# A third bank for the rows' sums, late inputs for two batches, 64-row transposes, and a new order at the last batch and the first two experts

## The chip, the cores and the metric

The kernel runs on one core of a Trainium2 chip. The metric is the device time of one execution in microseconds. Before the change the median of three runs is 163.81 us (163.64 to 164.35). About 0.5% (0.8 us) is the least change that a measurement of this kernel can tell.

## The reference

The input x has B = 8 batches of T = 128 tokens with C = 256 channels; a second input v has the same shape.

```python
x = x + wkv(time_decay, time_first, k=layernorm(x), v=ctx)   # a scan over tokens, each channel by itself
h = rmsnorm(layernorm(x)) * norm_w
scores = softmax(h @ gate_w.T)                # 32 experts
w, ids = top_k(scores, 4); w = w / sum(w)     # 4 experts for each token
routed = sum over the 4: w * (silu(h @ w13[e].gate) * (h @ w13[e].up)) @ w2[e]    # F = 128, at most 256 rows for each expert
out = x + layernorm(x) + routed + shared expert(h)
```

Inside wkv each channel keeps two running sums, of exp(k)*v and of exp(k), both decayed from token to token; its result is their quotient, with an extra weight on the token itself. Everything is fp32.

## The kernel before

**First half, batch after batch.** One batch passes through these steps. ScalarE forms `ek` = exp of the normalised x (`exp_k`, L472) and VectorE multiplies by v (`times_v`, L633). TensorE transposes both to channels (`to_channels`, L940). VectorE runs the scan (`scan`, L639) and forms numerator and denominator (`num_den`, L652). ScalarE forms the reciprocal as exp of minus a logarithm (`first_reciprocal`, L484 and L488). VectorE multiplies (`with_reciprocal`, `minus_quotient`, giving Y). TensorE puts x into a PSUM bank `YT` (`residual_in`, L950) and adds Y, turned back to tokens (`to_tokens`, L955). VectorE takes mean and variance of that bank (`stats`, `mean_var`, `variances`), ScalarE makes scale and shift of them (`shifts`, L495 to L503) and writes the normalised row (`normed`, L507) and the residual base (`base`, L512). TensorE transposes the normalised row (`normed_to_channels`, L964), ScalarE copies it (`normed_T`, L518), TensorE forms the logits (`logits`, L977), VectorE picks four experts and a one-hot table (up to `one_hot`), TensorE counts earlier picks (`slots_so_far`, `positions`, L984 to L993), and VectorE turns the counts into row numbers (`picked_slots`, `slot_sums`, `slot_numbers`, L722 to L733). GpSimd then scatters the batch's rows to DRAM with one indirect DMA for each of the four ranks (`scatter`, L370).

**What sets the order.** Each engine has its own list of (lag, stage) pairs, given to `run`: in round n it carries out each stage for batch n - lag, in the order of the list. So an engine in round n works on several batches at once, and a stage that waits holds up all that stands behind it on that engine. Nothing is reordered by the program; a wait is always on a semaphore that another engine counts up. Buffers come in pairs (index j = batch modulo 2), `YT` among them, and `residual_in` of batch b must wait until ScalarE has finished `base` of batch b - 2.

**Scales of the inputs.** Mean and variance of x are formed before its exponentials: VectorE's `first_stats` (L599, L602), ScalarE's `first_scales` (L452, L454), VectorE's `first_shift` (L594). They come in two groups, batches 0 and 1, then batches 2 to 7. The second group's statistics and shift stand in VectorE's round 0, and its scales in ScalarE's `exp_k` of batch 2, in that round too.

**SP queue.** SP issues all large loads: x, gate weights and v of batches 0 and 1; x and v of batches 2 to 7; eight transfers of 1056 KB that clear the experts' rows in DRAM (L259); the shared expert's weights (L263 to L265); expert weights. GpSimd's scatters of batch 0 wait for the first four clearing transfers, those of batch 1 for the others. An expert's rows are loaded back (`xg`, L273) when rank 0, 0 to 1, 0 to 2 or all ranks have landed, for experts 0, 1, 2 and the rest in the order of work. GpSimd scatters ranks 0 and 1 of the last batch before ranks 2 and 3 of the last two.

**Second half, expert after expert.** For each of 32 experts: TensorE transposes its gathered rows (`rows_to_channels`, L1041), ScalarE copies them (`rows_to_sbuf`, L539), TensorE forms gate and up (`gate_up`, L1055), ScalarE silu (L544), VectorE the product (`gated`, L867), TensorE the down product (`down`, L1072), VectorE copies the result out (L873 to L877), GpSimd scatters it (L384). Counts decide at run time, by branches on TensorE, how many rows an expert has: up to 128 (one half), up to 192 (`second` set) or up to 256 (`third` set too). VectorE carries bookkeeping between the first experts (`picks_of_single`, `picks_of_pair`, `late_picks`, `weights_in_order`). The shared expert's products (`shared_part`, L998; `shared_down`, L1031) lie between the halves. At the end the experts' rows are gathered back by rank, weighted and added.

## Time and profile before

| what | value |
|---|---|
| median of 3 runs | 163.81 us (163.64 to 164.35) |
| the profiled execution, its own time | 165.11 us |
| its span, first to last instruction | 163.3 us |
| TensorE busy | 135.1 us (83% of the span) |
| VectorE busy | 114.1 us (70%) |
| ScalarE busy | 91.4 us (56%) |
| GpSimd busy | 85.5 us (52%) |
| mean DMA rate | 285 GB/s |

The profiled execution took 165.11 us, of which 163.3 us is the span and 1.8 us lies around it. Busy shares are means over stages that differ: the batches take about the first 62 us, then come some 15 us of transition, the experts to 142 us, and the gathering to the end. In the rows below PE is TensorE, PEld its weight loads, DVE VectorE, ACT ScalarE, POOL GpSimd. An fp32 product counts as two records, an fp32 transpose as one. A record's length contains its latency, so that overlapping records are longer than the distance between their starts.

### The profile page before, as it was taken

The numbers are of one execution on the slowest core, as the hardware profiler recorded it, in microseconds if no ns is written. First come the engines' busy times: TensorE is split into PE (matmuls) and PEld (weight loads), VectorE is DVE, ScalarE is ACT, GpSimd is POOL, SyncE is SP. The second block draws the span as 40 slices with busy tenths as digits, with TensorE's granted clock in tenths as the row PEclk, the third lists the DMA queues.
The fourth block names the chain that finished last, engine by engine and source line by source line (L and its number), as shares of the span: only waits on it lengthen the run. The fifth ranks groups of instructions, "written<-read, shape, count | busy, mean of one in ns | idle before, by whom it ended". The sixth has DMA issues, their size and how long they took to land.

```text
span 163.3 us, 2856 instructions
## 1 busy us (share of the span) xinstructions
PE 135.1 (83%) x740; PEld 114.9 (70%) x740; DVE 114.1 (70%) x415; ACT 91.4 (56%) x262; POOL 85.5 (52%) x106
## 2 busy tenths in 40 slices
PE   0254598889886799597979999998999999999591
PEld 0233397879775787285869988987999989888350
DVE  0489989999998633516997788787766787734471
ACT  3623777877777624025847798887845776210011
POOL 8200004777777774720557767777664677671000
PEclk9999999999999999969999999999999999999999
DMA  4999999999999981679989999997766321285977
GB/s 103 288 379 420 420 417 412 385 382 370 375 382 373 373 293 72 151 218 291 365 250 332 381 351 377 366 342 237 209 197 166 118 87 64 69 308 180 354 270 257
DMA packets 32433, 46.49 MB, mean 285 GB/s; under 512 B 3017, under 2 KB 27285, under 8 KB 32156
## 3 DMA queue, kind: packets, MB, share of 16 engines
q1 hardware_dynamic: 27936, 37.15, 67.3%
q0 software_dynamic: 3888, 8.53, 14.4%
q10 hardware_dynamic: 588, 0.54, 1.0%
q8 instruction: 11, 0.18, 0.5%
q14 instruction: 10, 0.08, 0.1%
HBM read 27.95 MB, written 20.48 MB: 297 GB/s over the span
## 4 chain that ended last, share of the span: by engine, by line
PE 53%; DVE 15%; DMA 12%; ACT 9%; issue 6%; POOL 1%; ACTq 1%; SPq 0%; DVEq 0%; POOLq 0%
PE bank L1055 20%; PE bank L1072 11%; PE bank L1041 6%; DMA w_all<-rows_out 5%; DVE S L639 4%; DVE ND L652 2%; PE bank L940 2%; DMA rows_out<-w_all,pick_idx 2%; PE bank L977 2%; PE bank L964 2%; PE bank L955 2%; PE bank L950 2%; DMA xg<-rows_in 2%; ACT n_row L507 2%; ACT ln_den L484 2%
## 5 line engine op out<-in xcount | busy, mean ns | idle before, releaser
L384 POOL DMA_INDIRECT rows_out<-w_all,pick_idx x49 | 48.2, 985 | 28.9 <-DVE w_all L873 10.0
L370 POOL DMA_INDIRECT rows_in<-n_row,slot_all x32 | 32.7, 1023 | 32.3 <-DVE slot_all L733 21.5
L1055 PE MATMUL bank<-xT,w_all 128*128 128x128 f32 (+2 forms) x256 | 41.3, 305 | 1.5 <-issue 1.2
L1055 PEld LDWEIGHTS bank<-xT,w_all 128*128 128x128 f32 x256 | 36.1, 193 | 4.1 <-issue 3.7
L539 ACT ACTIVATE xT<-bank,nws 128x256 f32<-128x256 f32 x64 | 26.9, 471 | 14.9 <-PE bank L1041 14.6
L1072 PE MATMUL bank<-w_all,act_t 128*128 128x256 f32 x92 | 25.3, 382 | 1.0 <-DVE act_t L867 1.0
L867 DVE TENSOR_TENSOR act_t<-sg,bank 128x256 f32<-128x256 f32 x32 | 13.4, 419 | 13.7 <-ACT sg L544 13.6
L544 ACT ACTIVATE sg<-bank 128x256 f32<-128x256 f32 x32 | 12.3, 383 | 9.5 <-PE bank L1055 8.7
L1072 PEld LDWEIGHTS bank<-w_all,act_t 128*128 128x128 f32 x92 | 15.6, 191 | 2.5 <-issue 1.7
L1041 PE MATMUL bank<-ident,xg 128*128 128x128 f32 x92 | 15.8, 280 | 1.5 <-DMA xg<-rows_in 1.4
L1041 PEld LDWEIGHTS bank<-ident,xg 128*128 128x128 f32 x92 | 12.1, 143 | 5.4 <-issue 2.5
L873 DVE COPY w_all<-bank 128x512 f32<-128x512 f32 x17 | 11.7, 687 | 0.7 <-PE bank L1072 0.5
L998 PE MATMUL bank<-hT,sgu 128*128 128x256 f32 x32 | 11.5, 517 | 0.0
L914 DVE SCALAR_TENSOR_TENSOR base_all<-w_all,base_all 128x256 f32<-128x256 f32 x16 | 7.0, 482 | 5.5 <-DMA w_all<-rows_out 5.3
L484 ACT ACTIVATE ln_den<-ND,inv_top 128x128 f32<-128x128 f32 x16 | 5.6, 394 | 9.3 <-DVE ND L652 9.3
L955 PE MATMUL bank<-minus,Y 128*128 128x128 f32 x32 | 8.7, 425 | 2.4 <-DVE Y L669 2.4
L639 DVE TENSOR_TENSOR_SCAN S<-decay,bank 128x512 f32<-128x512 f32 x8 | 9.7, 1213 | 1.3 <-PE bank L940 1.3
L964 PE MATMUL bank<-ident,n_row 128*128 128x128 f32 x16 | 5.5, 448 | 5.5 <-ACT n_row L507 5.5
L1119 PE MATMUL bank<-w_all,v_all 128*128 128x256 f32 x32 | 8.4, 400 | 1.9 <-DMA w_all<-rows_out 1.8
L955 PEld LDWEIGHTS bank<-minus,Y 128*128 128x128 f32 x32 | 7.8, 333 | 2.8 <-DVE Y L669 2.8
L950 PE MATMUL bank<-x_all,ident 128*128 128x256 f32 x16 | 9.3, 686 | 0.0
L940 PE MATMUL bank<-ident,ek 128*128 128x128 f32 x16 | 5.4, 440 | 4.7 <-DVE ekv L633 4.7
(143 smaller groups left out, 228.7 us busy)
## 6 DMA issues: line engine op xcount, KB each, us to landing
w_all<-in_L_ffn_w_dram SPq DMA_DIRECT2D x12, 1024.0 KB, 14.3
rows_in<-w_all SPq DMA_DIRECT2D x8, 1056.0 KB, 16.1
xg<-rows_in SPq DMA_DIRECT2D x32, 264.0 KB, 4.7
w_all<-rows_out SPq DMA_DIRECT2D x2, 1024.0 KB, 5.4
w_all<-rows_out SPq DMA_DIRECT2D x2, 512.0 KB, 7.1
w_all<-rows_out SPq DMA_DIRECT2D x4, 256.0 KB, 8.0
rows_out<-w_all,pick_idx POOLq DMA_INDIRECT x49, 2.9
x_all<-in_x_dram SPq DMA_DIRECT2D x1, 768.0 KB, 6.1
```

The source lines that it names most:

```text
L370: pool.indirect_dma_start(rows_in, bass.IndirectOffsetOnAxis(ap=slot_all[:, b, k:k + 1], axis=0), n_row[:, b, :], None)\
L384: pool.indirect_dma_start(rows_out, bass.IndirectOffsetOnAxis(ap=pick_idx[:, e, a:a + 1], axis=0), yo[e][:, a, :], None, bounds_check=PICK ...
L539: last = act.activation(xT[:, j, h, :], FX[j][:, h, :], ACT.Copy, scale=nws[:, h:h + 1])
L544: act.activation(sg[:, j, :], FG[j][:, 0, :], ACT.Silu).then_inc(s["f_s"], 1)
L639: dve.tensor_tensor_scan(S[:, j].rearrange("p a h t -> p (a h t)"), decay[:, :, :, :].rearrange("p a h t -> p (a h t)"), XT[j].rearrange(" ...
L867: dve.tensor_tensor(act_t[:, j, :], sg[:, j, :], FG[j][:, 1, :], ALU.mult).then_inc(s["f_a"], 1)
L873: dve.tensor_copy(yo[e], FY[i % 2]).then_inc(s["f_yo"], 1)
L950: nc.tensor.matmul(YT[j], ident[:, :], x_all[:, b, :], start=True, stop=False)
L955: last = nc.tensor.matmul(YT[j][:, h * P:(h + 1) * P], Y[:, j, h, :], minus[:, :], start=False, stop=(h == HC - 1))
L1041: last = nc.tensor.transpose(FX[j][:, h, a * P:(a + 1) * P], xg[e % XB][:, a, h * P:(h + 1) * P], ident[:, :])
L1055: last = nc.tensor.matmul(FG[j][:, a, lo:lo + slots], w13_all[:, expert(e), h, a, :], xT[:, j, h, lo:lo + slots], start=(h == 0), stop=(h ...
L1072: return nc.tensor.matmul(FY[j][:, a, :], act_t[:, j, a * P:(a + 1) * P], w2_all[:, expert(e), :], start=True, stop=True)
```

## The change

Seven edits go together.

1. **Third bank.** `YT` gets banks 2, 3 and 5 (batch modulo 3), and the transposed normalised rows `NT` keep one bank instead of two. In TensorE's list `residual_in` moves from the head of the round (for batch n) to behind `positions` (for batch n + 1), and it now waits for `base` of batch b - 3.
2. **Late inputs.** x and v of batches 6 and 7 are loaded by two transfers of their own behind the eight clearing ones. Their statistics and shift move to VectorE's round 4, their scales to ScalarE's `exp_k` of batch 6.
3. **First exponential.** `exp_k` of batch 0 is issued right behind the first scales; VectorE's wait for all constants moves from before the first product to `num_den` of batch 0, and TensorE's wait for the gate weights to the first logits.
4. **Shifts.** In `shifts`, `nb2`, for which `normed` waits, comes before `one_rs2`, for which `base` waits.
5. **Last batch.** `to_tokens` of batch 7 comes before `normed_to_channels` of batch 6. Of the shared expert's products one stands before the last logits instead of two, and none before the last `positions` instead of one; those moved come later. Each half of the logits waits for its own half of the copied rows.
6. **First two experts.** TensorE transposes experts 0 and 1 and then forms gate and up of both; ScalarE copies both before its first silu. Half of the second `shared_down` moves ahead of the first transposes.
7. **64-row transposes.** Where an expert has 129 to 192 rows, the extra half is transposed as 64 rows, behind one more branch.

```diff
-        YT = [bank[2 + j][:, 0:C] for j in range(2)]
-        NT = [bank[4 + j][:, 0:C].rearrange("p (h t) -> p h t", h=HC) for j in range(2)]
+        YT = [bank[q][:, 0:C] for q in (2, 3, 5)]
+        NT = bank[4][:, 0:C].rearrange("p (h t) -> p h t", h=HC)
...
+            sp.dma_start(x_all[:, THIRD:B, :], xv[:, THIRD:B, :]).then_inc(s["x2_in"], 16)
+            sp.dma_start(v_all[:, THIRD:B, :], vv[:, THIRD:B, :]).then_inc(s["v2_in"], 16)
             sp.dma_start(sgu[:, :, 0, :], sh_gate.rearrange("(h p) f -> p h f", p=P)).then_inc(s["sh_in"], 16)
...
             first_scales(0, 0, FIRST)
+            def first_exp():
+                act.wait_ge(s["nb1_done"], 1)
+                act.activation(ek[:, 0, :], x_all[:, 0, :], ACT.Exp, bias=nb1[:, 0:1], scale=rstd1[:, 0:1]).then_inc(s["ek_ready"], 1)
+
+            first_exp()
...
             def exp_k(b, j):
+                if b == 0:
+                    return
                 if b == FIRST:
-                    first_scales(1, FIRST, B)
-                act.wait_ge(s["nb1_done"], 1 if b < FIRST else 2)
+                    first_scales(1, FIRST, THIRD)
+                if b == THIRD:
+                    first_scales(2, THIRD, B)
+                act.wait_ge(s["nb1_done"], 1 if b < FIRST else 2 if b < THIRD else 3)
...
             rows_to_sbuf(0, 0)
-            for e in range(E):
-                if e == 0:
-                    silu(0, 0)
+            rows_to_sbuf(1, 1)
+            silu(0, 0)
+            silu(1, 1)
+            for e in range(1, E):
...
             def others_shift(b, j):
                 if b == 0:
-                    first_shift(1, FIRST, B)
+                    first_shift(1, FIRST, THIRD)
+                if b == THIRD - 2:
+                    first_shift(2, THIRD, B)
...
             def to_tokens(b, j):
+                if b < B - 1:
+                    rows_of(b, j)
+
+            def last_to_tokens(b, j):
+                if b == B - 1:
+                    rows_of(b, j)
...
                     pe.wait_ge(s["sh_in"], 32)
-                    for h in range(HC):
-                        shared_part(0, 0, h)
-                pe.wait_ge(s["hT_ready"], HC * (b + 1))
+                    shared_part(0, 0, 0)
...
                 for h in range(HC):
+                    pe.wait_ge(s["hT_ready"], HC * b + h + 1)
                     last = nc.tensor.matmul(LG, hT[:, b, h, :], gwT[:, h, :], start=(h == 0), stop=(h == HC - 1))
...
-            run([(0, residual_in), (2, slots_so_far), (-1, to_channels), (2, positions), (1, normed_to_channels), (0, to_tokens), (1, logits)])
...
+            run([(2, slots_so_far), (-1, to_channels), (2, positions), (-1, residual_in), (0, last_to_tokens),
+                 (1, normed_to_channels), (0, to_tokens), (1, logits)])
+
+            shared_part(0, 0, 1)
...
-            for h in range(1, HC):
+            for h in range(HC):
+                shared_part(0, 1, h)
+            pe.wait_ge(s["base_ready"], B)
+            for h in range(HC):
                 shared_part(1, 0, h)
...
             pe.wait_ge(s["sdn_in"], 16)
-            shared_down(0)
+            shared_down(0, 0)
+            shared_down(0, 1)
+            shared_down(1, 0)
...
+            def transpose_rows(e, j, a, lo, hi):
                 for h in range(HC):
-                    last = nc.tensor.transpose(FX[j][:, h, a * P:(a + 1) * P], xg[e % XB][:, a, h * P:(h + 1) * P],
-                                               ident[:, :])
+                    last = nc.tensor.transpose(FX[j][:, h, a * P + lo:a * P + hi], xg[e % XB][lo:hi, a, h * P:(h + 1) * P],
+                                               ident[lo:hi, lo:hi])
                 return last
...
+                first_rows = (0, MORE - P) if more else (2 * P - MORE, P)
                 with pe.If(second != 0):
-                    transpose_half(e, j, extra(expert(e)))
-                transpose_half(e, j, main(expert(e))).then_inc(s["f_xt"], 1)
+                    with pe.If(third != 0):
+                        transpose_rows(e, j, more, 0, P)
+                    with pe.Else():
+                        transpose_rows(e, j, more, *first_rows)
+                transpose_rows(e, j, main(expert(e)), 0, P).then_inc(s["f_xt"], 1)
...
+            rows_to_channels(0, 0, second(0), third(0))
+            shared_down(1, 1)
+            rows_to_channels(1, 1, second(1), third(1))
+            gate_up(0, 0, second(0), third(0))
+            gate_up(1, 1, second(1), third(1))
+            for e in range(1, E + 1):
```

On TensorE, one round in the middle of the batches, before the change (`ek` and `ekv` are the exponentials and their products with v, `slot`, `earlier` and `onehot` belong to the counting):

```order
L950 MATMUL bank<-x_all,ident 128x256 [waits base_ready]
L984 MATMUL bank<-slot,ident 128x32 [waits earlier_done,picked_done]
L986 MATMUL bank<-earlier,ones 128x32 x4
L940 MATMUL bank<-ident,ek 128x128 [waits col0_done,nd_done,ekv_ready]
L940 MATMUL bank<-ident,ek 128x128
L940 MATMUL bank<-ident,ekv 128x128 x2
L993 MATMUL bank<-onehot,tri 128x32 [waits onehot_done]
L993 MATMUL bank<-onehot,tri 128x32 x3
L964 MATMUL bank<-ident,n_row 128x128 [waits hT_ready,n_ready]
```

and after it:

```order
L1013 MATMUL bank<-slot,ident 128x32 [waits earlier_done,picked_done]
L1015 MATMUL bank<-earlier,ones 128x32 x4
L958 MATMUL bank<-ident,ek 128x128 [waits col0_done,nd_done,ekv_ready]
L958 MATMUL bank<-ident,ek 128x128
L958 MATMUL bank<-ident,ekv 128x128 x2
L1020 MATMUL bank<-onehot,tri 128x32 [waits onehot_done]
L1020 MATMUL bank<-onehot,tri 128x32 x3
L970 MATMUL bank<-x_all,ident 128x256 [waits base_ready]
L992 MATMUL bank<-ident,n_row 128x128 [waits hT_ready,n_ready]
```

The product that brings x into the bank now stands behind the transposes of the next batch and the counting, directly ahead of the transposes of the normalised rows.

On VectorE in round 4 after the change, from the product with the reciprocal to the next scan (`nb` is the shift of batches 6 and 7 and is new here; before the change nothing stood between `slot_v` and `earlier`):

```order
L681 TENSOR_TENSOR NR<-ND,R 128x512 [waits y_ready,nd_done,r0_ready]
L741 TENSOR_TENSOR picked<-onehot,bank 128x128 [waits pos_ready]
L688 SCALAR_TENSOR_TENSOR Y<-NR 128x256 [waits x1_ready,nr_done]
L747 TENSOR_REDUCE slot_v<-picked 128x4 [waits picked_done]
L607 SCALAR_TENSOR_TENSOR nb<-mv,rstd 128x2 [waits rstd1_done,mv1_done]
L734 TENSOR_TENSOR earlier<-earlier,onehot 128x128 [waits pos_ready,onehot_done]
L752 SCALAR_TENSOR_TENSOR slot_all<-slot_v 128x4 [waits slot_v_done]
L656 SCALAR_TENSOR_TENSOR S<-decay,bank 128x512 [waits nd_done,xt_ready]
```

The shift waits for `rstd1_done`. ScalarE counts that up in the same round at this place (`hT` is the copy of the transposed normalised rows):

```order
L519 ACTIVATE n_row<-bank,nb,rs 128x256 [waits nb2_done]
L524 ACTIVATE base_all<-bank,nb,one_rs 128x256 [waits one_rs2_done]
L530 ACTIVATE hT<-bank,nws 128x128 [waits nt_ready]
L530 ACTIVATE hT<-bank,nws 128x128
L455 ACTIVATE ln_ve<-mv,eps 128x2 [waits mv1_done]
L457 ACTIVATE rstd<-ln_ve 128x2 [waits ln_ve1_done]
L484 ACTIVATE ek<-x_all,nb,rstd 128x256 [waits xt_ready,nb1_done]
```

So the two small instructions stand behind both halves of `hT` of batch 3.

## Rows read from the trace of the kernel before

**Rows 1.** Windows: length, busy PE, PEld, DVE, ACT, POOL, clock, DMA, GB/s.
```profile
36.50:41.95 5.45, 4.96 (x28) 4.46 (x27) 5.11 (x20) 4.26 (x14) 4.23 (x5) 1.00 1.08 376
...
70.00:72.00 2.00, 2.00 (x6) 1.27 (x5) 0.21 (x1) 0.84 (x2) 0.49 (x1) 0.50 0.50 187
...
77.00:150.00 73.00, 70.96 (x448) 63.63 (x447) 54.73 (x199) 46.79 (x121) 48.25 (x49) 1.00 0.75 243
```

**Rows 2.** Chain that ended last, kernel start: start us, us, what.
```profile
6.62 0.53 ACT ek L472
...
11.43 1.98 DVE st L599 x6
...
13.53 0.41 DVE mv L602 x5
```

**Rows 3.** Timeline, VectorE: start us, us, instruction; scans of batches 3 and 7.
```profile
25.63 1.21 DVE L639 TENSOR_TENSOR_SCAN S<-decay,bank 128x512 f32<-128x512 f32 x1
...
47.42 1.21 DVE L639 TENSOR_TENSOR_SCAN S<-decay,bank 128x512 f32<-128x512 f32 x1
```

**Rows 4.** The same chain, TensorE at 33 us: residual product.
```profile
33.07 1.01 PE bank L950 x2
```

**Rows 5.** Timeline around 34 to 37 us; in brackets idle before and releaser.
```profile
34.11 0.16 DVE L680 BATCH_NORM_AGGREGATE mv<-st 128x2 f32<-128x6 f32 x1
...
35.53 0.29 DVE L722 TENSOR_TENSOR picked<-onehot,bank 128x128 f32<-128x128 bf16 x1 [0.20 <-PE bank L993]
...
36.07 0.28 DVE L728 TENSOR_REDUCE slot_v<-picked 128x4 f32<-128x128 f32 x1
...
36.81 0.63 ACT L518 ACTIVATE hT<-bank,nws 128x128 f32<-128x128 f32 x2 [0.33 <-PE bank L964]
```

**Rows 6.** Timeline, ScalarE at the start: scales of batches 2 to 7.
```profile
13.97 0.30 ACT L452 ACTIVATE ln_ve<-mv,eps 128x6 f32<-128x6 f32 x1 [1.57 <-DVE mv L602]
...
14.30 0.21 ACT L454 ACTIVATE rstd<-ln_ve 128x6 f32<-128x6 f32 x1
```

**Rows 7.** Timeline, GpSimd: scatters of rows to the experts.
```profile
37.73 0.96 POOL L370 DMA_INDIRECT rows_in<-n_row,slot_all  x1 [0.30 <-issue]
...
60.29 0.96 POOL L370 DMA_INDIRECT rows_in<-n_row,slot_all  x1 [0.30 <-issue]
...
63.21 0.95 POOL L370 DMA_INDIRECT rows_in<-n_row,slot_all  x1 [1.96 <-issue]
```

**Rows 8.** Timeline, VectorE: row numbers of the last batch.
```profile
61.90 0.16 DVE L733 SCALAR_TENSOR_TENSOR slot_all<-slot_v 128x4 int32<-128x4 f32 x1
```

**Rows 9.** SP queue's timeline; then DMA table: KB each, us to landing.
```profile
15.45 2.35 SPq L263 DMA_DIRECT2D sgu<-L_ffn_shared_gate_w_dram  x1
...
sgu<-L_ffn_shared_gate_w_dram SPq DMA_DIRECT2D x1, 128.0 KB, 16.4
```

**Rows 10.** The chain again, TensorE in the last batch.
```profile
57.13 1.71 PE bank L998 x4
...
60.07 1.04 PE bank L998 x2
```

**Rows 11.** Timeline, TensorE and VectorE, where the experts start.
```profile
66.98 1.10 PE L1031 MATMUL bank<-sdn,act_t 128*128 128x256 f32 x4 [1.11 <-DVE act_t L754]
...
68.99 1.05 PE L1041 MATMUL bank<-ident,xg 128*128 128x128 f32 x4 [0.90 <-DMA xg<-rows_in]
...
74.24 0.44 PE L1041 MATMUL bank<-ident,xg 128*128 128x128 f32 x2 [0.45 <-DMA xg<-rows_in]
...
76.99 0.42 DVE L867 TENSOR_TENSOR act_t<-sg,bank 128x256 f32<-128x256 f32 x1 [0.83 <-ACT sg L544]
...
83.35 0.70 PE L1072 MATMUL bank<-w_all,act_t 128*128 128x256 f32 x2 [0.84 <-DVE act_t L867]
```

**Rows 12.** Timeline, TensorE, logits of one batch.
```profile
32.00 1.06 PE L977 MATMUL bank<-gwT,hT 128*128 128x32 f32 x4
```

**Rows 13.** Instructions by form, 68 to 143 us: busy us, mean ns | idle.
```profile
L1055 PE MATMUL bank<-xT,w_all 128*128 128x192 f32 x104 | 19.9, 335 | 0.4 <-issue 0.4
```

More of the change, by code:

```diff
@@ L235, in _ @@
             vv = ctx_in.rearrange("b t c -> t b c")
[L236 removed]
+            for lo, hi, x_in, v_in in ((0, FIRST, "x0_in", "v0_in"), (FIRST, THIRD, "x1_in", "v1_in")):
                 sp.dma_start(x_all[:, lo:hi, :], xv[:, lo:hi, :]).then_inc(s[x_in], 16)
@@ L1026, in third, with shared_down, rows_to_channels @@
                 return flags[1][expert(e) // BITS] & (1 << expert(e) % BITS)
-            def shared_down(c):
-                pe.wait_ge(s["sh_a"], c + 1)
-                for a in range(2):
-                    last = nc.tensor.matmul(FY[c][:, a, :], act_t[:, c, a * P:(a + 1) * P], sdn[:, :], start=True, stop=True)
-                last.then_inc(s["sh_y"], 1)
+            def shared_down(c, a):
+                if a == 0:
+                    pe.wait_ge(s["sh_a"], c + 1)
+                product = nc.tensor.matmul(FY[c][:, a, :], act_t[:, c, a * P:(a + 1) * P], sdn[:, :], start=True, stop=True)
+                if a == 1:
+                    product.then_inc(s["sh_y"], 1)
             pe.wait_ge(s["sdn_in"], 16)
-            shared_down(0)
+            shared_down(0, 0)
+            shared_down(0, 1)
+            shared_down(1, 0)
             pe.wait_ge(s["nd_done"], 2 * B)
             pe.wait_ge(s["idx_done"], B)
-            def transpose_half(e, j, a):
+            def transpose_rows(e, j, a, lo, hi):
                 for h in range(HC):
-                    last = nc.tensor.transpose(FX[j][:, h, a * P:(a + 1) * P], xg[e % XB][:, a, h * P:(h + 1) * P],
-                                               ident[:, :])
+                    last = nc.tensor.transpose(FX[j][:, h, a * P + lo:a * P + hi], xg[e % XB][lo:hi, a, h * P:(h + 1) * P],
+                                               ident[lo:hi, lo:hi])
                 return last
-            def rows_to_channels(e, j, second):
+            def rows_to_channels(e, j, second, third):
                 pe.wait_ge(xg_in[e % XB], 16 * (e // XB + 1))
+                more = extra(expert(e))
+                first_rows = (0, MORE - P) if more else (2 * P - MORE, P)
                 with pe.If(second != 0):
-                    transpose_half(e, j, extra(expert(e)))
-                transpose_half(e, j, main(expert(e))).then_inc(s["f_xt"], 1)
+                    with pe.If(third != 0):
[3 more added lines that the diff above has]
+                transpose_rows(e, j, main(expert(e)), 0, P).then_inc(s["f_xt"], 1)
             def gate_up_slots(e, j, slots):
@@ L1081, in down @@
                 down_half(e, j, main(expert(e))).then_inc(s["f_y"], 1)
-            rows_to_channels(0, 0, second(0))
-            shared_down(1)
-            for e in range(E + 1):
-                if e == 0:
-                    gate_up(0, 0, second(0), third(0))
+            rows_to_channels(0, 0, second(0), third(0))
[4 more added lines that the diff above has]
+            for e in range(1, E + 1):
                 if e + 1 < E:
-                    rows_to_channels(e + 1, (e + 1) % 2, second(e + 1))
+                    rows_to_channels(e + 1, (e + 1) % 2, second(e + 1), third(e + 1))
                 if e == 1:
```

60 lines of the change are left out of this document (31 added, 29 removed).

## The prediction

> **What bounds the kernel now.** I read the windows first, then the chain of waits, then the timeline where stages meet. Between 36.5 and 41.95 us one batch passes; VectorE is busy for 5.11 of 5.45 us, TensorE for 4.96, ScalarE for 4.26 [rows 1]. So VectorE is the bound of the batches, with 0.34 us of idle time in each. From 77 to 150 us TensorE is busy for 70.96 of 73 us [rows 1]. The four scans from batch 3 to batch 7 start 21.79 us apart, 5.45 for each batch [rows 3].
>
> Between the halves the chain goes through GpSimd. It issues the scatters at 37.73, ..., 60.29 us, with 17 others between, each with only 0.3 us idle before it, and then has a hole of 1.96 us before 63.21 [rows 7]. The last row numbers are written at 61.90 to 62.06 us, 1.15 us before that scatter starts [rows 7, 8]. The first expert's transposes start at 68.99 us, 5.78 after it [rows 11].
>
> **The change part by part.**
>
> *First exponential, -0.6.* It starts at 6.62 us [rows 2], after six small ScalarE instructions. Its shift is ready at about 5.9, so it can start at about 6.0. Bounds 0 and -0.7. The work now behind it is next needed at the first numerator, over 3 us later.
>
> *Fewer statistics at the start, -0.8.* The chain holds six of each kind, 1.98 + 0.41 = 2.39 us [rows 2]. A third of that goes.
>
> *Third bank, -1.5 by the scan of batch 7.* The product that brings x in costs 1.01 us on the chain [rows 4], between the logits and the transposes for a later batch. It moves to where TensorE waits for the normalised rows. VectorE's wait for the counts (0.20 us at 35.53 [rows 5]) then ends. VectorE itself can't go faster than about 5.15 us for each batch, so the gain is 5.45 - 5.15 = 0.3 for each of the five rounds from batch 2 to batch 7. Bounds 0 and -1.7 (5 times the idle 0.34). Putting `nb2` first saves 0.1 on a chain that is then hidden.
>
> *Late statistics, +0.85.* Two of each kind plus a shift return in round 4, on the engine that is the bound.
>
> *The late shift's wait, +1.9.* In round 4 VectorE's shift of batches 6 and 7 stands behind `slot_v` and waits for two ScalarE instructions that stand behind `hT` of batch 3. In the trace of before `mv` starts at 34.11 us, `slot_v` ends at 36.35 and `hT` at 37.44 [rows 5]. `hT` ends 3.33 after `mv`, and 0.1 less with `nb2` first. The late statistics stand ahead of `mv` and so move both. Logarithm and exponential take from 13.97 to 14.51, 0.54 us [rows 6]. So the scales are ready 37.34 + 0.54 = 37.88, and VectorE stands from 36.35 (36.2 without its other wait) to there: 1.6, plus 0.15 for the shift and 0.15 for handing over, 1.9. Behind it are `earlier`, the row numbers of batch 2 and the scan of batch 5. At the start the same pair cost nothing, since no `hT` stood before it. Bounds +1.0 and +2.2.
>
> Sum at the scan of batch 7: -0.6 - 0.8 - 1.5 + 0.85 + 1.9 = -0.15. What starts the batches early is given back in round 4.
>
> *Late inputs.* They take the place of the shared gate weights, which were issued at 15.45 us and landed 16.4 later, at 31.85 [rows 9]. 512 KB less stand in front and 256 KB of x are their own, so x lands at about 31. VectorE asks for it at about 31.5 (scan of batch 4 at 29.1, plus 2.4). I take 0; bounds 0 and +1.
>
> *Last batch, -1.3 to the last row numbers.* Two shared products (1.71 us) stand ahead of the last logits and one, 1.04 us with its neighbour, ahead of the last counts [rows 10]. Half of the first goes, 0.85, and some 0.3 of the second, since the counts' operands are ready soon after it starts. The early `to_tokens` gives 0.1 to 0.2: batch 7's statistics come 0.85 sooner, but its transposes wait behind the counts of batch 6, which come no sooner. With -0.15 from above the last row numbers come 1.45 sooner, at 60.6.
>
> *GpSimd.* Row numbers of batch 2 now come with the delayed scan of batch 5: 25.63 + 2 × 5.45 = 36.5 before, less 0.6 + 0.8 + 3 × 0.3, plus 2.75, is 37.0. Its first scatter starts about 1 us after, at 38.0, not 37.73. From that one to the end of the one at 60.29 it took 61.55 - 37.73 = 23.82 with the idle 0.3 [rows 7]. So the queue is free for the last batch at 61.8, and the row numbers of 60.6 + 1.15 allow 61.75. The scatter of 63.21 starts at 61.8: **-1.4**.
>
> *First experts.* With 5.78 us behind it the first expert's rows are there at 67.6. TensorE has more to do first. Seven shared products (0.855 each, half of 1.71) instead of five follow the last counts, and end at about 65.8 as before; 1.1 us of register loads follow, then three products instead of two. The two took 1.10 us from 66.98 [rows 11], so three end at about 68.2 and the transposes start there, -0.8. Then half a shared product instead of one whole and the second expert's two transposes lead to gate and up of expert 0, 1.2 to 1.4 sooner than before. VectorE's first wait for expert 1 (0.83 us before 76.99 [rows 11]) goes, because gate and up of expert 1 no longer stand behind the third expert's rows, which TensorE awaited until 74.24 [rows 11]. From there VectorE's bookkeeping bounds until 83.35, where TensorE waits for it the last time [rows 11]. So that point moves by 1.2 + 0.8 = **-2.0**. Bounds: 0 and -2.8. Behind it TensorE is the bound and unchanged.
>
> *64-row transposes, 0.* There are 104 / 8 = 13 experts with 192 columns [rows 13], 26 shorter transposes. An upper bound of the gain is half of each: 0.105 us a transpose (0.44 us for two less 0.23 of latency), so 26 × 0.05 = 1.4. But a transpose must also load 128 columns of weights. Logits with 32 moving columns take 1.06 us for four records, transposes with 128 take 1.05 for four [rows 11, 12], so the load sets their pace. I take 0, with the extra branch hidden by TensorE's queue; bounds -1.4 and +4.4 (below).
>
> The Trainium skill, "TensorE: Matmul & The Clock Gate", section "Back-to-back issue gap", says that a weight load's time follows the number of columns and not the rows contracted; by it too 26 halved transposes give 0 instead of 1.4, and these rows agree for columns, while none here shows 64 contracted rows in a dense stream.
>
> **Sum.** -2.0 for the profiled execution: 165.11 - 2.0 = 163.1. It ran 1.3 above the median of the runs, so that the forecast for the median is 163.81 - 2.0 = **161.8**.
>
> **Rivals.**
>
> A. *The late shift hardly stalls.* If ScalarE's pair finds its place in an idle stretch, the 1.9 stays saved. Against it speaks the fixed order. GpSimd's queue is then free earlier and the last row numbers lead: 1.7 more, 160.1.
>
> B. *The clock.* TensorE's granted clock is 0.50, that is 1.2 GHz, at 70 to 72 us [rows 1], after the idle time between 66 and 69; before 66 us the column says 1.00, but shared products take 0.43 us a record there [rows 10], against some 0.22 at 66.98 [rows 11], which is the pace of 1.2 GHz. It had been busy without a break before it rose. Moving products behind the last counts changes where it rises. If it rises only after the three `shared_down` products, these cost 1.3 more and gate and up of the first two experts run at half pace, so that VectorE's bookkeeping starts no earlier than now. Gain 0.2 to 0.6: 163.4. For it: the rise in before came at the very end of the products. Against it: the new unbroken stretch is longer, 6 us against 4.5.
>
> C. *Late x holds VectorE.* If x of batches 6 and 7 lands at 32.5, scan 5 and with it GpSimd's batch 2 come 1 us later: 162.8. The landing at 31.85 of what stood there [rows 9] speaks against more.
>
> D. *Slower: a drain at each change of the transposes' height.* If TensorE must empty before 64 rows follow 128 and again after, each change costs a latency. A lone pair of transposes takes 0.44 us and two in a stream 0.21, so up to 0.2; the nearest row gives 0.17 for 26 changes, 4.4 us, and the time is 161.8 + 4.4 = 166.2. It makes the change slower from 2.0 / 26 = 0.08 us a change. For it: TensorE has no slack there. Against it: no row shows such a change.
>
> The Trainium skill, "TensorEngine Tiling (Array Packing)", section "Key Properties", states that switching the tiling mode drains the engine; by it D would hold if 64 rows are such a mode, which no run here shows yet.
>
> **How the numbers follow.** Chances: forecast 0.50 (own range 161.0 to 162.6), A 0.17, B 0.15, C 0.08, D 0.10. The range 160.1 to 163.7 holds A, the forecast, C and most of B, some 0.85, and leaves D. Below 163.0 (faster by over 0.5%) (about what a measurement of this kernel can tell from no change) lie the forecast, A, C and a third of B, 0.80, less 0.02 for the forecast's own tail: 0.78. Within 0.5% (163.0 to 164.6) lie the rest of B, that tail and a mild D of 0.02: 0.14. Slower: the rest of D, 0.08.
>
> **What would show it.** Right: in round 4 VectorE idles for about 1.6 us before `nb`, released by ScalarE's `rstd`; rounds take about 5.15 us elsewhere; the hole before the last batch's scatter is gone and that scatter starts near 61.8; TensorE's last wait for VectorE's bookkeeping ends near 81.3; the experts behind it take as long as before. Wrong: no idle time at `nb` (A), a granted clock of 0.50 beyond 73 us (B), VectorE waiting for x near 31 us (C), or gaps of 0.1 us and more beside each 64-row transpose (D). A forecast of 161.8 fails outright if the stretch from 84 us to the end changes by more than 1 us.

## The result

| | median | ratio to before, 95% interval |
|---|---|---|
| before, same rounds | 163.72 us (163.08 to 164.35) | |
| changed | 166.00 us (164.98 to 166.41) | 1.013 (1.007 to 1.019) |

The change makes the kernel slower, by 1.3%. The forecast was 161.8 us. The profiled execution took 166.06 us with a span of 164.3, against 165.11 and 163.3 before. (Ratios here and below compare undisturbed executions alone, so they can differ a little from the quotient of two medians.)

First the windows of the changed kernel, with the columns of [rows 1]: one round of the batches, two stretches at the first experts, and the experts as a whole.

```profile
37.13:42.18 5.05, 3.29 (x18) 2.09 (x18) 5.05 (x22) 3.25 (x12) 3.58 (x3) 1.00 1.07 369
70.00:72.00 2.00, 1.59 (x7) 1.36 (x8) 0.35 (x1) 0.90 (x3) 0.00 (x0) 0.81 0.64 172
77.00:150.00 73.00, 71.33 (x437) 60.56 (x438) 52.97 (x197) 45.99 (x120) 48.30 (x49) 1.00 0.74 239
72.00:74.00 2.00, 2.00 (x9) 2.00 (x8) 0.12 (x1) 0.38 (x1) 0.00 (x0) 0.50 0.93 246
```

A round takes 5.05 us in place of 5.45, with VectorE busy throughout. The third bank was forecast to bring it to 5.15; no run isolates it from the other edits. The half clock (0.50, that is 1.2 GHz) has not gone. Before it held from 70 to 72 us; now it holds from 72 to 74 us, and the mean from 70 to 72 is 0.81, so that it fell inside that window.

VectorE's timeline, answering to [rows 3, 5, 8]: scans of batches 2, 3, 4, 5 and 7, the late statistics, and the late shift.

```profile
18.00 1.21 DVE L656 TENSOR_TENSOR_SCAN S<-decay,bank 128x512 f32<-128x512 f32 x1
...
23.34 1.21 DVE L656 TENSOR_TENSOR_SCAN S<-decay,bank 128x512 f32<-128x512 f32 x1
...
28.39 1.21 DVE L656 TENSOR_TENSOR_SCAN S<-decay,bank 128x512 f32<-128x512 f32 x1
31.44 0.75 DVE L612 BATCH_NORM_STATS2 st<-x_all 128x6 f32<-128x256 f32 x2 [0.59 <-DMA x_all<-in_x_dram]
...
36.81 0.16 DVE L607 SCALAR_TENSOR_TENSOR nb<-mv,rstd 128x2 f32<-128x2 f32 x1 [1.88 <-ACT rstd L457]
...
37.13 1.21 DVE L656 TENSOR_TENSOR_SCAN S<-decay,bank 128x512 f32<-128x512 f32 x1
...
47.23 1.21 DVE L656 TENSOR_TENSOR_SCAN S<-decay,bank 128x512 f32<-128x512 f32 x1
```

Batch 3 is scanned 2.29 us sooner than before, batch 7 only 0.19 (forecast 0.15). The scan of batch 2 came 1.50 us sooner; before, it was this one:

```profile
19.50 1.21 DVE L639 TENSOR_TENSOR_SCAN S<-decay,bank 128x512 f32<-128x512 f32 x1
```

Round 4 takes 8.74 us from the scan of batch 4 to that of batch 5: 5.05 as usual, 0.59 of waiting for x, 1.88 at the shift, and the remaining 1.22 for the late statistics and the shift. ScalarE shows why: its pair for batches 6 and 7 starts only behind `hT` of batch 3.

```profile
35.65 0.63 ACT L530 ACTIVATE hT<-bank,nws 128x128 f32<-128x128 f32 x2 [0.32 <-PE bank L992]
36.17 0.29 ACT L455 ACTIVATE ln_ve<-mv,eps 128x2 f32<-128x2 f32 x1
36.49 0.20 ACT L457 ACTIVATE rstd<-ln_ve 128x2 f32<-128x2 f32 x1
```

GpSimd, as in [rows 7]: its last batch starts at 62.15 us (63.21 before, forecast 61.8), after row numbers of 60.85 (61.90 before). The idle time before it, which was forecast to vanish, has only shrunk from 1.96 to 1.05 us.

```profile
62.15 0.96 POOL L373 DMA_INDIRECT rows_in<-n_row,slot_all  x1 [1.05 <-issue]
```

TensorE where the experts start, as in [rows 11]; 64x64 marks the transposes of 64 rows.

```profile
68.49 0.70 PE L1073 MATMUL bank<-ident,xg 64*128 64x64 f32 x4 [1.27 <-DMA xg<-rows_in]
69.03 0.60 PE L1060 MATMUL bank<-sdn,act_t 128*128 128x256 f32 x2
70.24 0.44 PE L1073 MATMUL bank<-ident,xg 128*128 128x128 f32 x2 [0.61 <-DMA xg<-rows_in]
70.85 4.11 PE L1092 MATMUL bank<-xT,w_all 128*128 128x192 f32 x16 [0.17 <-issue]
...
82.77 0.70 PE L1109 MATMUL bank<-w_all,act_t 128*128 128x256 f32 x2 [0.56 <-DVE act_t L886]
...
143.26 1.12 PE L1109 MATMUL bank<-w_all,act_t 128*128 128x256 f32 x4 [0.17 <-DVE act_t L886]
```

The transposes start 0.5 us sooner. TensorE then waits for the second expert's rows, and gate and up of both experts run for the most part at half clock, 4.11 us for 16 records. Its last wait for VectorE's bookkeeping ends at 82.77 us: 0.58 sooner, not 2.0. From there to the last down product it takes 60.49 us. Before it was 83.35 to the row below, 58.37 us.

```profile
141.72 1.12 PE L1072 MATMUL bank<-w_all,act_t 128*128 128x256 f32 x4 [0.17 <-DVE act_t L867]
```

So the balance is -0.58 up to that wait and +2.12 behind it, 1.54 later at 143.26 us; the stretch behind gives back 0.5, and the span is 1.0 longer. The medians lie 2.3 us apart and these two traces only 1.0, since the traced execution of before took 165.11 us, 1.4 above its median, and that of the changed kernel is at its median. Where those 1.4 us lie no trace shows.

### The profile page after: what moved, and what is told of

Its sections match the earlier page's. It is cut to its first block, busy times and chain, and to the rows that moved or that the text cites. A ratio compares the mean times of both kernels' runs of the same rounds, so it can differ in the third digit from the quotient of the medians.

```text
span 164.3 us, 2902 instructions
## 1 busy us (share of the span) xinstructions
PE 137.4 (84%) x740; PEld 111.2 (68%) x740; DVE 113.6 (69%) x416; ACT 91.1 (55%) x264; POOL 85.0 (52%) x106
## 4 chain that ended last, share of the span: by engine, by line
PE 52%; DMA 21%; SPq 8%; DVE 7%; issue 6%; POOL 2%; ACT 1%; POOLq 0%; DVEq 0%
PE bank L1092 22%; PE bank L1109 11%; DMA x_all<-in_x_dram 11%; PE bank L1073 7%; SPq L260 6%; DMA w_all<-rows_out 5%; DMA xg<-rows_in 2%; PE bank L1156 2%; DMA rows_out<-w_all,pick_idx 2%; PE bank L970 2%; POOL rows_in L373 2%; PE bank L983 2%; PE bank L1006 2%; DMA rows_in<-n_row,slot_all 1%; PE bank L992 1%
## 5 line engine op out<-in xcount | busy, mean ns | idle before, releaser
L387 POOL DMA_INDIRECT rows_out<-w_all,pick_idx x49 | 48.3, 986 | 31.5 <-DVE w_all L896 10.8
L373 POOL DMA_INDIRECT rows_in<-n_row,slot_all x32 | 32.2, 1007 | 31.7 <-DVE slot_all L752 22.1
L1092 PE MATMUL bank<-xT,w_all 128*128 128x128 f32 (+2 forms) x256 | 42.5, 312 | 1.7 <-issue 1.5
L1092 PEld LDWEIGHTS bank<-xT,w_all 128*128 128x128 f32 x256 | 37.2, 198 | 4.0 <-issue 3.7
L1073 PE MATMUL bank<-ident,xg 128*128 128x128 f32 (+1 forms) x92 | 16.8, 275 | 1.9 <-DMA xg<-rows_in 1.9
L1073 PEld LDWEIGHTS bank<-ident,xg 128*128 128x128 f32 (+1 forms) x92 | 10.5, 140 | 9.6 <-issue 7.3
L1025 PE MATMUL bank<-hT,sgu 128*128 128x256 f32 x32 | 10.3, 478 | 0.0
L1156 PEld LDWEIGHTS bank<-w_all,v_all 128*128 128x128 f32 x32 | 5.6, 189 | 4.0 <-DMA w_all<-rows_out 3.4
```

The lines of the kernel that those rows point to most:

```text
L373: pool.indirect_dma_start(rows_in, bass.IndirectOffsetOnAxis(ap=slot_all[:, b, k:k + 1], axis=0), n_row[:, b, :], None)\
L387: pool.indirect_dma_start(rows_out, bass.IndirectOffsetOnAxis(ap=pick_idx[:, e, a:a + 1], axis=0), yo[e][:, a, :], None, bounds_check=PICK ...
L1073: last = nc.tensor.transpose(FX[j][:, h, a * P + lo:a * P + hi], xg[e % XB][lo:hi, a, h * P:(h + 1) * P], ident[lo:hi, lo:hi])
L1092: last = nc.tensor.matmul(FG[j][:, a, lo:lo + slots], w13_all[:, expert(e), h, a, :], xT[:, j, h, lo:lo + slots], start=(h == 0), stop=(h ...
L1156: last = nc.tensor.matmul(FT[q], diag[:, q, r, :], G[r][:, 2 * q + 1, :], start=False, stop=(r == K - 1))
```

## The experiments

"The changed kernel" is the one that is explained here. Two chips ran all kernels, before too, at 182 us instead of 164, and ratios are to before on the same chip; times at 182 us are not compared with times at 164.

### Is it the height of the transposes?

**full_rows**: the changed kernel without edit 7.

```diff
-                first_rows = (0, MORE - P) if more else (2 * P - MORE, P)
                 with pe.If(second != 0):
-                    with pe.If(third != 0):
-                        transpose_rows(e, j, more, 0, P)
-                    with pe.Else():
-                        transpose_rows(e, j, more, *first_rows)
+                    transpose_rows(e, j, more, 0, P)
```

> The changed kernel with all transposes over 128 rows again and without the added branch. Theory S (each change between 64 and 128 rows on TensorE costs about 0.1 us, because the next weights are not loaded ahead): 26 changes or 2.6 us go, so 166.0 - 2.6 = 163.4, and the group of four transposes of an expert takes 0.44 us again, not 0.63. Rival C (the clock: the stretch of half clock at the first experts cost the time): still about 166.

**before_64**: the kernel before with edit 7 alone (the same lines added to it).

> The kernel before with the 64-row transposes and their branch alone. Theory S: 163.7 + 2.6 = 166.3, since TensorE is the bound from 84 to 142 us. Rival R (the loss comes from the other edits): 163.7.

**branch_only**: the changed kernel with the added branch, but 128 rows on either side of it.

```diff
-                first_rows = (0, MORE - P) if more else (2 * P - MORE, P)
+                first_rows = (0, P)
```

> The changed kernel with its added branch, but 128 rows in both arms. Theory S: as without 64 rows, 163.4. Rival N (the nested branch itself holds TensorE's queue): about 166, with four transposes still in 0.63 us.

Measured, all at 182 us: full_rows 0.984 (0.976 to 0.993), branch_only 0.990 (0.978 to 1.001), before_64 1.009 (1.004 to 1.014). The medians of all executions, which scatter over 4 to 8 us in each, are 181.77, 183.73 and 183.26 us, against 182.06. The heights with their branch cost the old kernel about 0.9%, and without them the changed kernel is no slower. The times leave the branch open. Its trace speaks against it: from a down product over four transposes to the next gate and up, branch_only takes 0.87 us where nothing else holds it up, as full_rows does without the branch.

```profile
132.03 0.59 PE L1109 MATMUL bank<-w_all,act_t 128*128 128x256 f32 x2
132.47 0.60 PE L1073 MATMUL bank<-ident,xg 128*128 128x128 f32 x4
132.90 1.47 PE L1092 MATMUL bank<-xT,w_all 128*128 128x192 f32 x8
```

With 64 rows at 182 us (after_again, before_64) no such group behind a down product of two records takes less than 1.06 us.

**full_rows_again**, on a chip at 164 us:

> The same kernel as full_rows, so that the three kernels beside it can be compared with it in the same rounds. Theory S (a price of about 0.1 us for each change between 64 and 128 rows, 26 changes): what is left of the change is worth the 0.6 us by which TensorE's last wait for the bookkeeping came sooner, a ratio to the kernel before of 0.990 to 0.999. Theory R (something else in the changed kernel, such as its first experts, costs the 2.3 us): 1.005 to 1.015.

Measured: 164.12 us against 163.98, ratio 0.999 (0.996 to 1.002). The six other edits together are worth nothing that can be measured. In its trace VectorE waits 1.41 us for x, the last batch's scatter starts at 62.90 us, only 0.31 sooner than before, and TensorE's last wait for the bookkeeping ends at 83.58, 0.23 later. That is a miss too, since the forecast had edit 7 at 0 and would have been 161.8 for this kernel as well.

**alternate** and **alternate_3**: the changed kernel with the order 64, 128, 64, 128 within an expert.

```diff
...
-                        transpose_rows(e, j, more, *first_rows)
-                transpose_rows(e, j, main(expert(e)), 0, P).then_inc(s["f_xt"], 1)
+                        for h in range(HC):
+                            transpose_part(e, j, more, *first_rows, h)
+                            last = transpose_part(e, j, main(expert(e)), 0, P, h)
+                        last.then_inc(s["f_xt"], 1)
...
```

The main half's transposes of all other experts move into branches of their own.

> The changed kernel, where an expert of 129 to 192 rows alternates: 64 rows, 128, 64, 128 instead of 64, 64, 128, 128. Four changes an expert instead of two, as many transposes. Theory S: 26 changes more at 0.1 us, 166.0 + 2.6 = 168.6. Rival I (each 64-row transpose costs more by itself, wherever it stands): 166.0.

> The changed kernel with 52 changes of height in place of 26. Theory S (price on the change): 2.6 to 3.3 us above after_3. Theory T (price on the 64-row transpose): within 0.5 us of it. The traces of alternate already show 0.25 us more for each 192-column expert.

> The changed kernel again, beside alternate_3 and early_scales_2. Theory S: 26 changes of height cost 2.7 us and the late scales 1.9 us, of which 1.3 to 2.0 reach the end, so it is 4.0 to 4.7 us above early_scales_2, ratio to before 1.010 to 1.018.

Measured: alternate 186.69 us, ratio 1.021 (1.011 to 1.030), beside 0.984 for full_rows. In one set of rounds at 164 us: after_3, the changed kernel, 166.38 us, 1.010 (1.005 to 1.015); alternate_3 168.69 us, 1.030 (1.026 to 1.033). (The same two kernels at 182 us, after_again and alternate_again, gave 1.007, 1.001 to 1.013, and 1.017, 1.006 to 1.028.) By the medians the 26 more changes cost 2.3 us, by the ratios 0.0196 × 164 = 3.2; theory T's bound of 0.5 us is excluded. The traces give the price of one change directly. TensorE's timeline of the same expert in full_rows_again (0 changes), after_3 (2) and alternate_3 (4): down product, four transposes, next gate and up.

```profile
97.76 0.60 PE L1105 MATMUL bank<-w_all,act_t 128*128 128x256 f32 x2
98.19 0.60 PE L1073 MATMUL bank<-ident,xg 128*128 128x128 f32 x4
98.63 1.06 PE L1088 MATMUL bank<-xT,w_all 128*128 128x128 f32 x8
```

```profile
95.96 0.60 PE L1109 MATMUL bank<-w_all,act_t 128*128 128x256 f32 x2
96.49 0.71 PE L1073 MATMUL bank<-ident,xg 64*128 64x64 f32 x4
97.04 1.11 PE L1092 MATMUL bank<-xT,w_all 128*128 128x128 f32 x8
```

```profile
97.47 0.60 PE L1118 MATMUL bank<-w_all,act_t 128*128 128x256 f32 x2
97.99 1.00 PE L1078 MATMUL bank<-ident,xg 64*128 64x64 f32 x4
98.83 1.15 PE L1101 MATMUL bank<-xT,w_all 128*128 128x128 f32 x8
```

From the down product to gate and up it takes 0.87, 1.08 and 1.36 us: 0.21 for the first two changes, and 0.28 more for the two that alternating adds, so 0.10 to 0.14 for each. In each of the three traces the groups of this kind in the dense stretch agree within 0.05 us, but for one in after_3 and one in alternate_3, while an expert without 64 rows takes the same in all three (1.08 us behind a down product of four records). So the branches of alternate_3 are not the cause.

Of the 13 experts with two changes, 11 lie in the dense stretch behind TensorE's last wait for the bookkeeping. One of the other two stands behind the wait for the first rows, the other (at 78.43 us in the changed kernel) before that last wait, so that VectorE and not TensorE sets the time there. With 0.20 us a group, the difference of the medians (1.07 and 0.87), 11 × 0.20 = 2.2 us reach the time, and the changed kernel's trace has 2.12 more there than the trace of before. From that wait to the last down product full_rows_again, after_3 and alternate_3 take 57.75, 59.72 and 63.06 us: 2.0 more for 22 changes, and 3.3 more for another 22 (11 × 0.28 = 3.1).

The weight loads say how. First the loads of the same four transposes in full_rows_again and in after_3, then after_3's loads by form between 83 and 143 us (busy us, mean ns | idle before them).

```profile
97.98 0.57 PEld L1073 LDWEIGHTS bank<-ident,xg 128*128 128x128 f32 x4
```

```profile
96.49 0.47 PEld L1073 LDWEIGHTS bank<-ident,xg 64*128 64x128 f32 x4 [0.33 <-issue]
...
L1073 PEld LDWEIGHTS bank<-ident,xg 128*128 128x128 f32 x52 | 6.4, 141 | 2.2
L1073 PEld LDWEIGHTS bank<-ident,xg 64*128 64x128 f32 x22 | 2.2, 137 | 3.6 <-issue 3.6
```

Without a change of height the loads begin at 97.98, 0.21 us before their first product (98.19), beside the down product. With one they begin together with it, at 96.49, after 0.33 us of idle time with nothing to wait for; this happens 11 times (22 loads, 3.6 us). And a load of 64 rows takes 137 ns, one of 128 rows 141, so that halving the rows saves nothing there.

### Is it ScalarE's order that holds the late shift?

**early_scales**: full_rows with the scales of batches 6 and 7 right behind the first reciprocal.

```diff
-                if b == THIRD:
-                    first_scales(2, THIRD, B)
...
+            def late_scales(b, j):
+                if b == THIRD - 2:
+                    first_scales(2, THIRD, B)
...
-            run([(0, first_reciprocal), (1, shifts), ...
+            run([(0, first_reciprocal), (0, late_scales), (1, shifts), ...
```

> full_rows, with ScalarE's two scales for batches 6 and 7 moved from behind the transposed copies of batch 3 to right behind the first reciprocal of that round. If VectorE's 1.9 us before the shift come from the place of this pair in ScalarE's order (the prediction's step), they go, the scan of batch 7 comes 1.7 to 1.9 us sooner than in full_rows, and GpSimd's first scatter too. The time is then 0.5 to 1.3 us below full_rows (the first expert's rows were awaited for 1.27 us in the changed kernel; ratio to full_rows 0.992 to 0.997). Rival: the wait is taken over by another one of the same round (x of batches 6 and 7, or the first exponential): no difference within 0.3 us, scan of batch 7 moved by under 0.5 us.

> The kernel of early_scales again, as the base of filled_waits_2. Ratio to the kernel before 0.983 to 0.993, as measured once; gate and up of the first two experts at a granted clock of 0.50.

Measured: 162.12 us, 0.988 (0.983 to 0.992), 2.0 below full_rows_again; once more (**early_scales_2**, beside after_3) 161.47 us, 0.979 (0.975 to 0.984), which is 4.9 below after_3, 0.2 more than expected, and below the ratio expected, 0.983 to 0.993. One of the six executions of early_scales took 243.97 us; it has no trace. VectorE's timeline of early_scales: the late statistics, then the scans of batches 5 and 7.

```profile
32.23 0.75 DVE L614 BATCH_NORM_STATS2 st<-x_all 128x6 f32<-128x256 f32 x2 [1.41 <-DMA x_all<-in_x_dram]
...
35.95 1.21 DVE L658 TENSOR_TENSOR_SCAN S<-decay,bank 128x512 f32<-128x512 f32 x1
...
46.04 1.21 DVE L658 TENSOR_TENSOR_SCAN S<-decay,bank 128x512 f32<-128x512 f32 x1
```

In full_rows_again, with the same 1.41 us of waiting for x, these scans start at 37.90 and 47.99, 1.95 us later: the shift's whole wait, 1.87 us there, is gone, and nothing takes its place. Last row numbers (61.59 to 59.61), last scatter (62.90 to 60.91) and first transposes (68.67 to 66.75 us) follow it. I had expected at most 1.3 us at the end, since TensorE's shared products stood in the way; but they stand behind the last counts and came sooner with them. early_scales is faster than both kernels.

**no_late_inputs**: full_rows without edit 2 (its lines of the diff undone).

> full_rows without the late inputs of batches 6 and 7: one transfer, one set of statistics and one shift for batches 2 to 7, as in the kernel before. By the prediction's steps the scans start 0.8 us later at first and 0.85 + 1.9 us are saved in round 4, with the 0.6 us of waiting for x seen in the changed kernel: scan of batch 7 2.0 to 2.6 us sooner than in full_rows, the time 0.5 to 1.3 us below it. Rival: the later gate weights and the larger first transfer hold the shared products or the early batches back, and the time is the same or up to 0.8 us above full_rows.

Measured: 163.69 us, 0.989 (0.982 to 0.997). That is 0.4 us below full_rows_again by the medians and 1.4 by the profiled executions. The scan of batch 7 starts at 44.55 us, 3.4 sooner, and the last row numbers are there at 58.13. But GpSimd does not keep up:

```profile
33.06 1.37 POOL L371 DMA_INDIRECT rows_in<-n_row,slot_all  x1 [2.42 <-DMA rows_in<-w_all]
...
60.05 0.96 POOL L371 DMA_INDIRECT rows_in<-n_row,slot_all  x1 [0.30 <-issue]
```

It waits until 33.06 us for the cleared rows (31.46 in full_rows_again), since more of x stands ahead of the clearing transfers, and from there its queue has no gap over 0.31 us up to the last batch at 60.05. So the late transfers have a use, an earlier clearing by 1.6 us. early_scales, whose scans come early as well, is the faster of the two kernels; that it owes this to the clearing is a reading of the traces, and no run tests it alone.

### The first two experts: order, rows and clock

**old_experts**: full_rows with the old order of the first two experts on TensorE (below) and, in the same way, on ScalarE.

```diff
             rows_to_channels(0, 0, second(0), third(0))
             shared_down(1, 1)
-            rows_to_channels(1, 1, second(1), third(1))
             gate_up(0, 0, second(0), third(0))
+            rows_to_channels(1, 1, second(1), third(1))
-            gate_up(1, 1, second(1), third(1))
```

> full_rows with the order of the first two experts on TensorE and ScalarE as it was: gate and up of expert 0 before the transposes of expert 1, and gate and up of expert 1 behind those of expert 2. By the prediction's step (the new order takes away VectorE's first wait for expert 1) it is 0.8 to 1.4 us above full_rows. By the clock theory (gate and up run at half clock in either order, and this sets the pace until TensorE's last wait for the bookkeeping) it is within 0.4 us of full_rows.

Measured: 164.62 us, 1.002 (0.998 to 1.005), 0.5 above full_rows_again: between the two expectations, and unclear. In its profiled execution x landed late and VectorE stood for it for 3.85 us, 2.44 more than in full_rows_again, which fits its 167.02 us, 2.4 above the median.

**filled_waits** and **filled_waits_2**: early_scales, with needless products in TensorE's two waits for rows.

```diff
+            def idle_products(n):
+                for _ in range(n):
+                    nc.tensor.matmul(bank[6][:, 0:C], ident[:, :], sdn[:, :], start=True, stop=True)
...
+            idle_products(3)
             rows_to_channels(0, 0, second(0), third(0))
             shared_down(1, 1)
+            idle_products(5)
```

> early_scales (ratio 0.988), with three needless identity products on TensorE before the first expert's transposes and five before the second's, which fill its waits of 0.8 and 1.2 us for gathered rows. Clock theory: the idle time of these waits lets the clock fall to half for gate and up of the first two experts (4.1 us); filled, they run at full clock in 2.1 us, VectorE's bookkeeping starts 1 to 2 us sooner, TensorE's last wait for it ends 1 to 2 us sooner, and the ratio falls by 0.006 to 0.012, to 0.976 to 0.982. Rival 1: the clock falls in spite of them, and the time is that of early_scales or up to 0.5 us more. Rival 2: the clock stays, but the bookkeeping starts by the rows of the second and third expert and not by gate and up: same time within 0.4 us with a granted clock of 1.00.

> The kernel of filled_waits again, beside early_scales in the same rounds. In its profile the clock stayed at 1.00 and gate and up of the first two experts took 2.45 us for 4.1. Clock theory: TensorE's last wait for VectorE's bookkeeping ends 1 to 2 us sooner than in early_scales_2, and the ratio of the two times is 0.988 to 0.994. Rival: the bookkeeping starts by rows that come later anyway, and the two times agree within 0.4 us.

Measured: filled_waits 181.96 us, 0.996 (0.990 to 1.001), on a chip at 182 us and without its base; filled_waits_2 161.56 us, 0.987 (0.984 to 0.989), beside early_scales_2 with 161.47 us and 0.979. TensorE's timeline of early_scales_2 and of filled_waits_2: second expert's transposes, gate and up, last wait for the bookkeeping.

```profile
69.09 0.44 PE L1075 MATMUL bank<-ident,xg 128*128 128x128 f32 x2 [0.95 <-DMA xg<-rows_in]
69.71 4.04 PE L1090 MATMUL bank<-xT,w_all 128*128 128x192 f32 x16 [0.18 <-issue]
...
81.54 0.70 PE L1107 MATMUL bank<-w_all,act_t 128*128 128x256 f32 x2 [0.69 <-DVE act_t L888]
```

```profile
70.01 0.38 PE L1079 MATMUL bank<-ident,xg 128*128 128x128 f32 x2
70.22 1.47 PE L1094 MATMUL bank<-xT,w_all 128*128 128x192 f32 x8
71.93 1.16 PE L1094 MATMUL bank<-xT,w_all 128*128 128x128 f32 x8 [0.24 <-issue]
...
80.72 0.70 PE L1111 MATMUL bank<-w_all,act_t 128*128 128x256 f32 x2 [0.70 <-DVE act_t L888]
```

Filled, the granted clock stays at 1.00 and gate and up are done 0.66 us sooner (73.09 against 73.75), though they start 0.51 later; the last wait ends 0.82 sooner. The traced execution of early_scales_2 was its slowest, 162.70 us; that of early_scales, 161.86 us, shows the same, 4.11 us for gate and up and a last wait that ends at 81.49. In filled_waits, too, the clock stayed at 1.00 (2.45 us). So the traces support that the idle time lets the clock fall.

The last wait was expected to end 1 to 2 us sooner. Part of the rest is the filling itself: in early_scales_2 the second expert's transposes start at 69.09, as soon as its rows are there, and in filled_waits_2 only at 70.01, with no idle time before them, behind the needless products. And the gain did not reach the time: 161.56 against 161.47 us by the medians, and by the ratios (0.987 and 0.979) it is no better. Why is open.

The changed kernel itself shows the clock's price, for in after_3's profiled execution the clock stayed up without any filling:

```profile
69.59 0.44 PE L1073 MATMUL bank<-ident,xg 128*128 128x128 f32 x2 [0.68 <-DMA xg<-rows_in]
70.26 2.47 PE L1092 MATMUL bank<-xT,w_all 128*128 128x192 f32 x16 [0.23 <-issue]
...
81.24 0.70 PE L1109 MATMUL bank<-w_all,act_t 128*128 128x256 f32 x2 [0.54 <-DVE act_t L886]
```

2.47 us instead of 4.11, and 1.53 sooner at the last wait (81.24 against 82.77), where 0.65 of it was there already at the second expert's transposes (69.59 against 70.24). That execution took 164.25 us; of the other five one took 164.35 and four 166.2 to 167.0. Such a gap is what a clock that falls in some executions and not in others would give, but only one of them has a trace, so this is not shown.

## Why the prediction was wrong, step by step

- **64-row transposes, 0.** This is the first step that failed. I had named the mechanism as rival D with 0.10 and refused it because no row of before showed a change of height; its turning point, 0.08 us a change, is just below the 0.10 to 0.14 that the traces show. Its sign came true (0.1 us beside each group of 64-row transposes), and so did the sign of failure, since the stretch behind the last wait changed by 2.12 us. Measured: 2.2 us for the 22 changes that count by the traces; after_3 less full_rows_again, on another chip, gives 1.8 us by the ratios (1.010 and 0.999) and 2.3 by the medians, and alternate's further 26 changes cost 2.3 to 3.2. Rival D's own price, 4.4 us, was twice too high. The Trainium skill, "TensorEngine Tiling (Array Packing)", section "Key Properties", states that changing the tiling mode drains TensorE, and a cost at every change fits that. The traces show the weight load, not issued ahead, as the place; whether TensorE drains there they do not show. The half of the step on loads was right: 137 against 141 ns. (The sentence on weight loads stands in the Trainium skill, "TensorE: Matmul & The Clock Gate", in section "LDWEIGHTS (loading the stationary operand)" and not in the one that the prediction names.)
- **First experts, -2.0; got -0.58.** The second step that failed, mis-sized by three things. The first transposes came 0.5 sooner and not 0.8. I let the second expert's transposes follow at once, but its rows come only at 70.24 us, and with the new order gate and up of expert 0 stand behind them. And the clock fell there (rival B's half pace), which costs 0.9 to 1.5 us at the last wait by after_3. It is why edit 7 is not the whole miss: without the 64-row transposes, in full_rows_again, that wait ends no sooner than before, the traced execution is 0.8 us below that of before (164.29 against 165.11) where 2.0 were forecast, and the medians are level.
- **First exponential and fewer statistics, -1.4.** Right: the scan of batch 2, up to which the sum has only these two, came 1.50 sooner.
- **Third bank, -1.5.** Right in kind, but mis-sized. The five rounds to the scan of batch 7 came 6.13 - 5.34, 5.50 - 5.05, 5.34 - 5.05, 5.49 - 5.05 and 5.46 - 5.05 us shorter (round 4 without its extra work), 2.4 us in all and beyond my bound of 1.7. Rounds took 5.05 us for 5.15, and the first two gained more than the mean idle time that I had taken for each.
- **Late statistics +0.85, late shift's wait +1.9.** The wait was right: 1.88 of idle time before the shift, released by ScalarE, and early_scales took all of it away by moving two instructions. The statistics with the shift took 1.22.
- **Late inputs, 0.** Mis-sized. VectorE asked for x at 30.85 us, sooner than the 31.5 that I took, and waited 0.59 us in the changed kernel, 0.50 to 1.41 in the six other traces at 164 us that have the late inputs and an ordinary wait, and 3.85 in old_experts: rival C's mechanism.
- **Their sum.** That the sum at the scan of batch 7 came out as forecast (-0.19 for -0.15) is luck: -1.50 - 2.38 + 1.22 + 0.59 + 1.88, in which the third bank's 0.9 more made up for the late statistics and the late x.
- **Last batch and GpSimd, -1.3 and -1.4.** The last row numbers came 1.05 sooner and the scatter 1.06. From the scan of batch 7 on the last batch gained 0.86 (1.05 less 0.19) where I had 1.3. Between the scatters of 37.73 and 60.29 us stand 16 others in the trace of before, not 17; the sum does not use the number.

## What to carry to other kernels

Count the changes of an operand's height in a dense TensorE stream, not its rows: a shorter transpose saved nothing in its load, and each change between 128 and 64 rows cost 0.10 to 0.14 us. When work is moved to a later round, its partner on the other engine must move to where it is ready, or the wait eats the gain: two small ScalarE instructions were worth 2.0 us, more than the six edits together. And putting one expert's product behind another expert's rows ties it to the later transfer, as the trace of the changed kernel shows; going back to the old order did not pay either (old_experts).

## What was unexpected of the hardware

- The same code ran gate and up of two experts at half clock in one execution, in 4.11 us (behind idle times of 1.27 and 0.61 us), and at full clock in another, in 2.47 us (behind 0.56 and 0.68). Of the seven traces at 164 us with this order and no filling, the clock also fell in full_rows_again (0.78 and 1.35), early_scales (0.80 and 1.20), early_scales_2 (1.33 and 0.95) and no_late_inputs (1.99 and 1.29), and also stayed in alternate_3 (0.74 and 0.34).
- The clock column does not always give the pace. From 30 to 40 us it says 1.00 in the changed kernel's trace and 0.50 in after_3's, and yet the same records last equally long in both: 704 ns where x comes into the bank, 444 ns for the transposes of `ek`. What the clock costs was read here from the lengths of records.
- On two chips every kernel took 18 us more. In filled_waits there all engines stood still together: between 41.30 us (a scatter of GpSimd's) and 43.47 nothing started on any engine. VectorE's next row and ScalarE's name no releaser in the kernel:

```profile
43.65 0.29 DVE L743 TENSOR_TENSOR picked<-onehot,bank 128x128 f32<-128x128 bf16 x1 [3.50 <-remote]
43.71 0.62 ACT L532 ACTIVATE hT<-bank,nws 128x128 f32<-128x128 f32 x2 [2.44 <-remote]
```

What held them is not in the profile.
